# A four-batch attention kernel: xn and half of LayerNorm 2 on ScalarE, its weight and residual in 1024-column operations on VectorE, the maxima split behind their transpose, later max rows issued by SyncE

## The reference, cut to what matters

```python
x = x + attn(layernorm(x), wq, wk_down, wv_down, wk_up, wv_up, wo)   # causal softmax attention
h = layernorm(x)
x = x + layernorm(h + outs) * ln_g + ln_b   # outs: expert-choice attention over rows picked from h
```

## Time and profile before

| | us |
|---|---|
| median of 3 runs (lowest, highest) | 525.21 (523.63, 525.84) |
| the profiled execution's own time | 527.11 |
| its span | 525.3 |
| busy: TensorE, VectorE, POOL, ScalarE | 458.1, 327.0, 233.9, 224.5 |
| mean granted clock of TensorE | 0.908 of full speed |

### The profile page before, as it was taken

One profiled execution on the slowest core, in us unless ns is written; L12 is line 12 of the kernel. 1 busy time (PEld: TensorE's weight loads), 2 busy tenths in 40 slices (PEclk: granted clock), 3 DMA queues, 4 the chain that ended last, 5 costly groups with the idle time before them and its releaser, 6 DMA issues.

```text
span 525.3 us, 7082 instructions
## 1 busy us (share of the span) xinstructions
PE 458.1 (87%) x2624; PEld 258.6 (49%) x2624; DVE 327.0 (62%) x500; ACT 224.5 (43%) x424; POOL 233.9 (45%) x180
## 2 busy tenths in 40 slices
PE   2886879899999799999999899999997998899671
PEld 1463556444756455545654464446564554434230
DVE  5256584767557977877468887844578568500524
ACT  1202225345464534644555345544544454446410
POOL 3000140336633943474428546454329443654752
PEclk9997586799999889999999799989997998688987
DMA  7399600037005510074034300290055100100002
GB/s 252 59 181 144 178 3 1 3 53 99 2 1 77 75 43 3 0 132 61 2 51 69 75 1 2 70 122 2 3 75 75 42 3 0 41 1 2 1 9 72
DMA packets 20867, 27.37 MB, mean 52 GB/s; under 512 B 3040, under 2 KB 13024, under 8 KB 20704
## 3 DMA queue, kind: packets, MB, share of 16 engines
q1 hardware_dynamic: 18976, 25.44, 27.3%
q10 hardware_dynamic: 1856, 1.48, 1.0%
HBM read 6.72 MB, written 4.19 MB: 21 GB/s over the span
## 4 chain that ended last, share of the span: by engine, by line
PE 64%; DVE 15%; DMA 5%; issue 5%; ACT 5%; POOL 3%; SPq 1%; ACTq 1%; POOLq 1%; DVEq 0%
PE st_ps L442 13%; PE u_ps L486 11%; PE mx_ps L463 11%; PE sh_ps L497 8%; DVE mx_part L809 5%; PE sh_ps L563 5%; DVE y L890 4%; PE sh_ps L531 4%; PE mx_ps L469 3%; DMA qs<-q_lo 3%; ACT pr L673 2%; PE sh_ps L536 2%; PE sh_ps L524 2%; DMA lnb<-in_ln_b 2%; DVE y L899 2%
## 5 line engine op out<-in xcount | busy, mean ns | idle before, releaser
L809 DVE TENSOR_REDUCE mx_part<-mx_ps 128x2 f32<-128x1024 f32 (+3 forms) x160 | 176.5, 1114 | 91.9 <-PE mx_ps L469 48.3
L673 ACT ACTIVATE pr<-st_ps 128x512 f32<-128x512 f32 (+1 forms) x304 | 168.5, 574 | 151.3 <-PE st_ps L442 143.7
L1072 POOL TENSOR_TENSOR pr<-pr 128x768 f32<-128x768 f32 (+3 forms) x72 | 154.9, 2156 | 70.2 <-ACT pr L673 68.3
L442 PE MATMUL st_ps<-qs,ks 98*128 98x512 f32 (+1 forms) x304 | 141.7, 482 | 8.7 <-ACT pr L673 5.6
L463 PE MATMUL mx_ps<-ks,qs 96*128 96x512 f32 (+3 forms) x384 | 118.3, 390 | 18.1 <-DVE mx_part L809 16.5
L1059 POOL TENSOR_SCALAR_AFFINE_SELECT pr<-pr 128x512 f32<-128x512 f32 x64 | 42.6, 666 | 157.4 <-ACT pr L673 155.0
L442 PEld LDWEIGHTS st_ps<-qs,ks 98*128 98x128 f32 x304 | 60.1, 203 | 92.6 <-ACT pr L673 45.3
L486 PE MATMUL u_ps<-pr,v 128*32 128x512 f32 (+3 forms) x768 | 90.9, 548 | 7.9 <-POOL pr L1059 7.9
L463 PEld LDWEIGHTS mx_ps<-ks,qs 96*128 96x128 f32 x384 | 75.2, 210 | 36.9 <-DVE mx_part L809 19.1
L469 PE MATMUL mx_ps<-mask_r,ident_r 128*128 128x128 f32 (+2 forms) x176 | 48.0, 272 | 0.0
L497 PE MATMUL sh_ps<-pr,ones 128*32 128x512 f32 (+1 forms) x384 | 42.1, 574 | 0.0
(11 more groups left out here) (80 smaller groups left out, 322.5 us busy)
## 6 DMA issues: line engine op xcount, KB each, us to landing
qs<-q_hi SPq DMA_DIRECT2D x32, 256.0 KB, 5.6
qs<-q_lo SPq DMA_DIRECT2D x16, 256.0 KB, 6.7
out_y<-y SPq DMA_DIRECT2D x8, 512.0 KB, 3.0
x<-in_x SPq DMA_DIRECT2D x3, 1024.0 KB, 13.9
ks<-k_hi SPq DMA_DIRECT2D x32, 64.0 KB, 5.4
x<-in_x SPq DMA_DIRECT2D x4, 256.0 KB, 4.1
pr<-in_wq ACTq DMA_DIRECT2D x1, 1024.0 KB, 7.8
pr<-in_wo SPq DMA_DIRECT2D x1, 1024.0 KB, 10.4
```

The costliest lines, as they stand in the source:

```text
L442: nc.tensor.matmul(st_ps[n % 2][:, 0:nh * width], ks[g][0:KM, kt * P:(kt + 1) * P], qs[g][0:KM, c, h0:h0 + nh, off:CH], start=True, stop=T ...
L673: nc.scalar.activation(pr[:, slot, h0:h0 + nh, off:CH], st_ps[n % 2][:, 0:nh * width].rearrange("p (h q) -> p h q", h=nh), ACT.Exp, scale= ...
L809: nc.vector.tensor_reduce(mx_part[:, t // CT, own, h0:h0 + nh, t % CT], mx_ps[n % 2][:, 0:nh * pitch].rearrange("p (h k) -> p h k", h=nh)[ ...
L1072: last = nc.gpsimd.tensor_tensor(even, even, pr[:, 6 + (e // 2) % 2, h0:h1, off:CH], ALU.add)
```

## The change

- ScalarE makes the 8 tiles of xn of the next batch, two after each of tiles 0 to 3 of window 0 (`normal`), as x * rstd + shift with shift = -mean * rstd. The first batch's stay on VectorE.
- ScalarE makes x * rstd + shift of LayerNorm 2 as well (`half`, 4 operations per chunk), after tiles 1 and 8 of window 0. VectorE multiplies by ln_g (`scale_half`) and adds x1b (`add_half`) in one operation each of 1024 columns.
- GpSimd computes the shifts, with two more small operations in each `rsqrt1` and `rsqrt2`. `rsqrt2` of chunk 0 moves from the end of window 1 to its tile 9.
- The maxima are transposed as they are. ScalarE's copy out of PSUM negates and rounds them (mx_hi), and VectorE makes the low part out of PSUM (`low_max`). `both_max` joins the two partial maxima of chunk 1.
- SyncE issues all max rows but the first two (`put_rows`). The output of chunk 1 is issued after the stacking of tile 11's q rows instead of before the first stacking.

```diff
-APPLY0, APPLY0_END = 10, 1
-APPLY1 = 7
+HALF0_AT, HALF1_AT = 1, 8
+SCALE_AT = [(2, 0), (9, 0)]
+ADD_AT = [(3, 0), (10, 2)]
+RSQRT1_AT, BIAS1_AT = 6, 7
+RSQRT0_AT, BIAS0_AT = 9, 11
...
+                put_rows(w, 1, use_no(b, 0, kind, "m1"))
                 if kind != FIRST:
                     put(b - 1, 0)
+                put_rows(w + 1, 0, use_no(b, 0, kind, "m0"))
+                if kind == LAST:
                     put(b - 1, 1)
+                    put_rows(w + 1, 1, use_no(b, 1, kind, "m1"))
+                    return
...
+                if kind != FIRST:
+                    put(b - 1, 1)
+                put_rows(w + 1, 1, use_no(b, 1, kind, "m1"))
+                put_rows(w + 2, 0, use_no(b, 1, kind, "m0"))
...
+            def put_rows(w, c, n):
+
+                sp.wait_ge(mx_hi_ready, w * NC + c + 1)
+                sp.dma_start(row_of(w, c, 0), mx_hi[:, :].bitcast(F)).then_inc(rows_in, 16)
+                sp.wait_ge(sh_read, n + 1)
+                sp.dma_start(row_of(w, c, 1), mx_lo[:, :].bitcast(F)).then_inc(rows_in, 16)
...
-                    pe.wait_ge(max_ready, wn * NC + 1 if c == 0 else w * NC + 2)
-                    last = nc.tensor.transpose(bank[0:2 * HG * CT, 0:P],
-                                               mx_split[:, :, :, :].rearrange("p a h t -> p (a h t)").bitcast(F),
-                                               ident[:, :])
+                    if c == 0:
+                        pe.wait_ge(mx_free, wn * NMX + MX_C0)
+                        m = mx_part[:, 0, 1, :, :]
+                    else:
+                        pe.wait_ge(max_ready, w + 1)
+                        m = mx_all[:, :, :]
+                    last = nc.tensor.transpose(bank[0:HG * CT, 0:P], m.rearrange("p h t -> p (h t)"), ident[:, :])
...
+                    nc.scalar.activation(mx_hi[:, :], bank[0:HG * CT, 0:P], ACT.Copy, scale=-1.0).then_inc(mx_hi_ready, 1)
...
+            def normal(b, t):
+
+                if t == 0:
+                    act.wait_ge(shift1_ready, NC + b)
+                nc.scalar.activation(xn[:, t, :], x[:, b, t, :], ACT.Identity, bias=shift1[:, b, t:t + 1],
+                                     scale=rstd1[:, b, t:t + 1]).then_inc(xn_ready, 1)
+
+            def half(b, c):
+
+                act.wait_ge(shift2_ready, b * NC + c + 1)
+                if b or c:
+                    act.wait_ge(out_done, 16 * (b * NC + c))
+                for t in range(CT):
+                    last = nc.scalar.activation(y[:, t, :], x[:, b, c * CT + t, :], ACT.Identity, bias=shift2[:, t:t + 1],
+                                                scale=rstd2[:, t:t + 1])
+                last.then_inc(half_ready, 1)
...
+                        if g == 0 and e < 4 and kind != LAST:
+                            normal(b + 1, 2 * e)
+                            normal(b + 1, 2 * e + 1)
+                        if g == 1 and kind == LAST and e == NE - 1:
+                            half(b, 0)
+                        if g == 0 and kind != FIRST and e in (HALF0_AT, HALF1_AT):
+                            half(b - 1, (HALF0_AT, HALF1_AT).index(e))
...
-            def split_max(w, c, uses_done):
-
-                dve.wait_ge(mx_free, w * NMX + (NMX if c else MX_C0))
-                if not (isinstance(uses_done, int) and uses_done == 0):
+            def both_max(w, uses_done):
+
+                dve.wait_ge(mx_free, w * NMX + NMX)
+                if uses_done:
                     dve.wait_ge(sh_full, uses_done)
-                m = mx_part[:, 0, 1, :, :]
-                if c:
-                    nc.vector.tensor_tensor(mx_all[:, :, :], mx_part[:, 1, 0, :, :], mx_part[:, 1, 1, :, :], ALU.max
-                                            ).then_inc(mx_step, 1)
-                    dve.wait_ge(mx_step, w * 3 + 2)
-                    m = mx_all[:, :, :]
-                nc.vector.tensor_scalar(mx_split[:, 0, :, :], m, -1.0, None, ALU.mult).then_inc(mx_step, 1)
-                dve.wait_ge(mx_step, w * 3 + (3 if c else 1))
-                nc.vector.scalar_tensor_tensor(out=mx_split[:, 1, :, :], in0=m, scalar=-1.0,
-                                               in1=mx_split[:, 0, :, :].bitcast(F), op0=ALU.mult, op1=ALU.subtract
-                                               ).then_inc(max_ready, 1)
+                nc.vector.tensor_reduce(mx_all[:, :, :].rearrange("p h t -> p (h t)"),
+                                        mx_part[:, 1, :, :, :].rearrange("p o h t -> p (h t) o"), AX.X, ALU.max
+                                        ).then_inc(max_ready, 1)
...
+            def low_max(w, c, n):
+
+                bank = sh_ps if n is not None else start_bank("m0")
+                done = sh_read if n is not None else start_sem("m0")
+                dve.wait_ge(sh_full, start_full("m0") if n is None else sh_fills(n))
+                dve.wait_ge(mx_hi_ready, w * NC + c + 1)
+                nc.vector.scalar_tensor_tensor(out=mx_lo[:, :], in0=bank[0:HG * CT, 0:P], scalar=-1.0,
+                                               in1=mx_hi[:, :].bitcast(F), op0=ALU.mult, op1=ALU.subtract).then_inc(done, 1)
...
-            def norm2_apply(b, c, powers, steps, t, last_half):
-
-                if not last_half:
-                    if t == 0:
-                        dve.wait_ge(out_done, y_count(b, c) * 16)
-                        dve.wait_ge(var_ready, powers)
-                    last = nc.vector.scalar_tensor_tensor(out=y[:, t, :], in0=x[:, b, c * CT + t, :], scalar=mv2[:, t, 0:1],
-                                                          in1=lng[:, :], op0=ALU.subtract, op1=ALU.mult)
-                    if t == CT - 1:
-                        last.then_inc(ln_step, 1)
...
-                last = nc.vector.scalar_tensor_tensor(out=y[:, t, :], in0=y[:, t, :], scalar=rstd2[:, t:t + 1],
-                                                      in1=x1b[:, t, :], op0=ALU.mult, op1=ALU.add)
-                if t == CT - 1:
-                    last.then_inc(y_ready, 1)
+            def scale_half(b, c):
+
+                dve.wait_ge(half_ready, b * NC + c + 1)
+                nc.vector.tensor_tensor(y[:, :, :], y[:, :, :], lng[:, None, :].to_broadcast([P, CT, D]), ALU.mult
+                                        ).then_inc(y_step, 1)
+
+            def add_half(b, c):
+
+                dve.wait_ge(x1b_ready, b * NC + c + 1)
+                dve.wait_ge(y_step, b * NC + c + 1)
+                nc.vector.tensor_tensor(y[:, :, :], y[:, :, :], x1b[:, :, :], ALU.add).then_inc(y_ready, 1)
...
             def rsqrt2(count, step):
 
                 pool.wait_ge(var_ready, count)
+                if count > 1:
+                    pool.wait_ge(shift2_ready, count - 1)
+                    pool.wait_ge(half_ready, count - 1)
+                nc.gpsimd.tensor_scalar(neg2[:, :], mv2[:, :, 0], -1.0, None, ALU.mult)
                 nc.gpsimd.tensor_scalar(var2[:, :], mv2[:, :, 1], 1.0 + EPS, EPS * EPS, ALU.mult, ALU.add).then_inc(pool_step, 1)
                 pool.wait_ge(pool_step, step)
                 nc.gpsimd.tensor_tensor(rstd2[:, :], var2[:, :], minus_half[:, 0:CT], ALU.pow).then_inc(rstd_ready, 1)
+                pool.wait_ge(rstd_ready, count)
+                nc.gpsimd.tensor_tensor(shift2[:, :], neg2[:, :], rstd2[:, :], ALU.mult).then_inc(shift2_ready, 1)
...
+                        if g == 0 and kind != FIRST:
+                            if e == RSQRT1_AT:
+                                pows += 1
+                                powers += 1
+                                rsqrt2(powers, pows)
+                            if e == BIAS1_AT:
+                                add_bias(b - 1, 1, use_no(b, g, kind, "f3") + 1)
+                        if g == 1:
+                            if e == 2 and b + 2 < B:
+                                pows += 1
+                                rsqrt1(b + 2, 0, TT, 2 * NC + b + 2, pows, NC + b + 2)
+                            if e == RSQRT0_AT:
+                                pows += 1
+                                powers += 1
+                                rsqrt2(powers, pows)
+                            if e == BIAS0_AT:
+                                add_bias(b, 0, use_no(b, g, kind, "f1") + 1)
```

134 lines of the change are left out of this document (65 added, 69 removed).

## The result

The changed kernel takes 535.83 us (median of 4 runs, 532.97 to 538.98); the kernel before took 525.53 beside it (523.63 to 526.23). The ratio is 1.020 (95% interval 1.013 to 1.027): slower by 2%, where 510 us and a gain were forecast. A ratio with an interval leaves out the runs that took over 1.5% longer than the fastest of their kernel; medians are over all runs.

What follows compares the result with a forecast made beforehand. TensorE was taken as the bound. Gains of 15.8 + 2.8 + 10.2 + 11.6 + 1.6 less costs of 7.1 + 2.1 + 2.0 + 2.8 gave 28.0 us; less 13.6 of clock, 14.4 from 525.2: forecast 510 us, range 495 to 521.

Steps and rivals of the forecast that it cites:

- Start of window 0: Batches 1 to 3: ScalarE's xn block and VectorE's multiply delay TensorE's transpose 2.7, 2.7 and 1.7 us; cost 7.1 us.
- the clock: Sign in the profile after: a mean clock above the 0.908 of before.
- Locks of the long operations: Tiles 9 and 10: scale_half and add_half meet GpSimd's additions and delay clearings; cost 0.7 us per batch, 2.1 in all.
- Small ones: sum1 waits for low_max (0.4 us twice), rsqrt1's new operations delay the clearing of tile 3 (0.6 twice); cost 2.0 us.
- Maxima: Batch 0: TensorE waits of 3.25 and 2.44 us go, with 10.1 us of clock behind them; gain 15.8 us.
- ScalarE's DMA issues: Window 1 of three batches: a 0.54 us wait goes as ScalarE no longer issues DMAs; gain 1.6 us.
- the stacking: Window 0: the wait for the late stacking of q, queued behind the output, goes; gain 1.22 us.
- End of the batches: Batches 0 to 2: waits of 2.60 us go, new ones of 1.66 come; gain 2.8 us, plus 10.2 of clock.
- X: Mean clock cost of each of six new TensorE waits: 2.3 us, 13.6 in all, with bounds 0 and 6.8.
- The end: Last batch: rsqrt2 adds 1.8 us to the last chain, operations behind the last variance 1.0; cost 2.8 us.
- the slower one: Rival: ScalarE's block at the start of window 0 holds TensorE until the clock falls and stays low; 538 us, chance 0.09.
- The change doesn't do what it says: Rival: the reduction of the maxima still waits for GpSimd; 521 us, within the smaller-gain case of 515 to 522, chance 0.13.

Runs made afterwards that it cites:

- g1: e6 with x + b and VectorE's addition of chunk 1 put back to steps 7 and 10, as in the change; 506.2 us.
- e6: Changed kernel with the moves of e1, e3 and e4, rsqrt1 at step 4 of window 1, last batch's rsqrt2 of chunk 0 behind all clearings; 494.0 us, 0.956.
- y1: e6 with VectorE's addition of chunk 1 alone put back to tile 10, x + b staying early on GpSimd; 493.3 us.
- e1: Changed kernel with GpSimd's x + b of chunk 1 at step 6 and VectorE's addition of chunk 1 at tile 9; 526.1 us.
- g2: e6 with rsqrt1 of batch b + 2 back at step 2 of window 1; 500.9 us.
- r1: Changed kernel with rsqrt1 of batch b + 2 at step 4 of window 1 instead of step 2; 532.1 us, ratio 1.023.
- x1: e6 with the maxima part taken back, the output of chunk 1 still behind the first stackings; 503.6 us.
- m1: Kernel before with the maxima part alone, its rows and the later output of chunk 1 issued by SP; 519.4 us, ratio 1.003.
- e3: Changed kernel with rsqrt2 and x + b of chunk 0 back at the end of window 1, except in the last batch; 524.3 us, 1.003.
- e4: Changed kernel with ScalarE's four operations of chunk 0 behind tile 4, VectorE's multiply and addition at tile 7; 528.2 us, ratio 1.012.
- y2: g1 with the clearing of tile 10 ahead of the second pair addition of tile 7 on GpSimd; 517.7 us, ratio 0.992.
- a0: The changed kernel run again, unaltered; 538.0 us, ratio 1.030 to the kernel before.
- e2: Changed kernel with VectorE's addition x + b + y made as four operations of 256 columns instead of one of 1024; 544.1 us.

## Why the prediction was wrong, point by point

The forecast was a gain of 15 us; it is a loss of 10. Three terms of the sum were mis-sized by some 18 to 31 us together (an estimate from medians of different runs), against the 26 between 510 and 535.8; the start of window 0, priced some 6 us too high, lies on the other side. Of the forecast's own signs, the clock failed: four runs of the changed kernel had 0.896 to 0.914, around the 0.908 of before and not above it.

*Locks of the long operations* were taken at 0.7 us per batch, 2.1, with "one addition", 2.4 a batch, as the upper bound. This step failed: `add_half` is not kept out by one addition but, when it comes at the wrong moment, until GpSimd pauses, 4.9 us beyond its own 1.23. I had looked at what GpSimd loses, and not at what stands behind VectorE. Measured: 12.3 us (g1 against e6), 12.9 (g1 against y1), 10 to 12 (e1); 8 to 11 us of the miss. The cause that I had not followed is the move of x + b to step 7, which shifts the chain behind it (y1) and in batch 3 stands ahead of a clearing that TensorE needs. The trace of before had the pattern, but not the length: in the earlier trace rows, 5.17 us for four operations beside GpSimd's.

The Trainium skill (SBUF — State Buffer, SBUF: two separate sides) has the lock held for the whole instruction. The trace agrees on that: in y1, GpSimd's addition of 1.81 us took 3.04, longer by about VectorE's whole 1.21. It shows more: the waiting side can miss its turn at several instruction ends, five of them in the 6.17 us.

*Small ones* put 0.6 us each on the clearing of tile 3, without clock. Against the 0.96 and 0.72 us of before, the waits grew by 0.3 and 0.5, less than forecast; what failed is the clock left out: the two places cost 6.9 us (g2; r1's 4 to 6 are not clear of the spread). Less the 1.7 us of waits that the kernel before had there and the 1.2 forecast, that is some 4 of the miss, or 2.5 if the 6.9 is taken from the ratios to the kernel before (0.966 and 0.956). At these two places waits of 1.17 to 1.29 us cost clock in most executions and those of 0.96 and 0.72 us in none; it is no threshold that this proves, since x1 had three waits of 1.15 us and its clock stayed at 1.00 from 108 to 418 us.

*Maxima*, with ScalarE's DMA issues and the stacking, was the largest gain, 18.6 us. Measured: 2.6 us by medians alone (m1), not to be told from zero, and 9.6 us, without the stacking's 1.2, in a kernel where the other moved pieces no longer wait (x1); 8 to 16 us of the miss. The mechanism was right: `mx_all` (16 columns) took 0.19 us at most, and `mx_lo` 0.28. The size was off in two steps: the new waits for `mx_lo` and `mx_all` (3.4 us in m1, 0.9 in after) were set at nothing, and the clock's 10.1 us came from one execution, on the costly side. Runs of the kernel before reach from 513 to 532 us, with mean clocks from 0.946 to 0.899; mine had 527.1 and 0.908.

What held: *End of the batches*, new waits of 1.66 forecast, 1.74, 1.73 and 1.60 measured; with clock 3 x (1.66 + 1.7) = 10.1 forecast, 11.5 to 14 measured (e3). *Start of window 0*, 2.7, 2.7 and 1.7 forecast, 2.64, 2.64 and 1.66 measured; with clock 7.1 + 8.5 = 15.6 forecast, 8 to 10 measured (e4). So X, 2.3 per new wait, was not too low: (12 - 5.1) + (9 - 6.9) over six waits is 1.5, or 1.8 with 14 in place of the 12; both are estimates from medians. The four and six ScalarE operations took 2.06 and 3.0 us, as taken. *The end*: a wait of 3.47 us where before had 1.98, and 1.28 behind it where before had 1.71, 1.1 more together against 1.8.

The rivals: the slower one gave 538 us, close to what came, but that is chance, since its mechanism is another; without the block at the start of window 0 (e4) the kernel is still not faster than before. "The change doesn't do what it says" was rightly held to be unlikely. The gains of the LayerNorm part itself were real, but only visible without its new waits: m1 to e6, 25 us, and x1, which has this part and not the maxima's, is 16 us below the kernel before beside it (0.974, 0.968 to 0.979). Both e6 and x1 have the moved pieces, so this is the part as re-placed.

Open is when exactly a waiting VectorE operation gets its turn. At 216.56 it came in the middle of a pair addition and got in ahead of the x + b behind it (1.75 us); at 223.21 and 342.07 it came 0.3 us before the end of one and did not, nor in y2 at 219.01, whatever followed. In batch 3 of y1 (412.94) it came in a pair addition with a clearing behind it and got in at the addition's end (2.65 us); the clearing was stretched to 1.62 us. Open too is how the 8 to 16 us missing from the maxima part divide between clock and waits, since each profile is one execution.

## What to carry to other kernels

Ask of every two-input operation that is put on VectorE what GpSimd does then, and whether it pauses: the wait can last for the whole chain up to the next pause, and what counts is who stands behind the operation. Small operations put ahead of something that TensorE waits for cost more than their length when the clock falls behind the wait. Take the clock's losses from several executions before they are booked as a gain; and try a change that adds several waits with its pieces moved before it is dropped, since this one was 2% slower as it stood and 4.4% faster with the places of its pieces altered.

## What the runs showed of the hardware

A VectorE operation of 256 columns with two SBUF operands, 0.42 us alone, took 5.35 us, across several GpSimd instructions, and splitting the long one did not help (e2). The reverse case also occurs: GpSimd's addition was stretched from 1.81 to 3.04 us and VectorE's took its plain 1.21 (y1). The clock's loss behind one and the same wait was 0 in one execution and 5 to 7 us in another (131.65 in a0, 130.19 in after). Identical code spread over 18 us (the kernel before, 513 to 532), with mean clocks from 0.946 to 0.899. One run of r1 took 620 us at a mean clock of 0.64, where its other five took 527 to 534; it is the run whose profile was kept.
